# A new order for four engines between attention tile 4 and the first expert gathers

## The chip, the core and the metric

One Trainium2 chip, one of its cores. The core's engines are PE (TensorE, the matrix products), DVE (VectorE), ACT (ScalarE), POOL (GpSimd) and SP (SyncE, which only issues transfers here). Each runs its own list of instructions strictly in order, and semaphores tie the lists together. The metric is the device time of one execution in microseconds (us), as the median of several runs.

## The reference: cross-attention, then a mixture of experts

`x` is (2, 512, 128), 1024 tokens of 128 numbers; `ctx` is (2, 77, 128).

```
x = x + xattn(layernorm(x), ctx, W_q, W_kv, W_out, gamma, beta)     # 16 heads of 64
    xn  = layernorm(x) * gamma + beta
    q   = xn @ W_q / 8 ;  k, v = split(ctx @ W_kv)
    out = softmax(q k^T) v  per head, joined, @ W_out
x = x + ffn(layernorm(x), ...)                                      # 8 experts, top 2, d_ff 512
    probs = softmax(x @ Wg + bg);  the two largest per token, normalized to sum 1
    out   = sum over the two experts e of
            w_e * ((silu(x @ W1[e] + b1[e]) * (x @ W3[e] + b3[e])) @ W2[e] + b2[e])
```

All is float32. The kernel computes an expert only for the tokens that chose it.

## The kernel before

**Tiles.** The tokens form T = 8 tiles of 128, TB = 4 for each of the two batches. The weights are folded first: scores are `xn_tile @ g` (16 heads times 77 context rows, 1232 columns, 3 PSUM banks), and attention's output is `prob @ vo` with 1232 rows in CH = 10 chunks of 128.

**A tile of attention.** `score_mm(t)` (PE) writes the scores into banks 0 to 2 (even t) or 3 to 5 (odd t). DVE takes the negative maximum (L728) and subtracts (L733, semaphore `s_sub`), which frees the banks; ACT does the exponential (`exps`, L578); DVE sums and inverts (`sums`, L721, L724); POOL multiplies (L476, `s_norm`). PE transposes the ten chunks in groups of four, four and two (keys `("pT", t, i)`, L1246, `st_mm`); ACT copies each group into `probT[:, t % 2]` (L595, L598, `st_free`); PE multiplies the ten chunks with `vo` (L1261; float32 products show as two instructions each, 20 a tile) into a bank `y`. For tiles 0 to 4 ACT copies `y` out (L560) and POOL adds it to x (`add_x`, L468); for tiles 5 to 7 DVE adds it from PSUM (`add_direct`, L763) and takes the statistics at once.

**PSUM.** The list `stage` names everything that goes through banks 7 and 6 in turn: `pT` of a tile, then `y`. Tiles 5 and 6 have their `y` in banks 3 and 4 (`Y_OWN`). `open_stage` waits until ACT has emptied what was in a bank before.

**The router** works on three groups of tiles: 0 to 3, 4 to 5, 6 to 7. For group n:
- statistics of x2 (`ln_stats`, DVE), then `rstd_step(4 + n)` on POOL (an add, L456, and a power, L458);
- `tokens_x2T(n)` (PE, L1156) transposes x2, ACT copies (`empty_x2T`, L566), `logits(n)` (PE, L1165) multiplies with the centred router weights `wg_c`. The router's means and the expert biases are two small PE operations at the head of `tokens_x2T(0)`;
- on DVE `shifts(n)` (L770), `top_two(n)` (L778 to L793: logits, maxima, indices, masks, and `sel`);
- `count_ranks(n)` (PE, L1174 to L1181) counts, per expert, the tokens ahead of each one;
- on DVE `ranks(n)` (L801), `blocks_of(n)` (L811 to L815) and `one_hots(n)` (`perm`, L822).
- ACT writes the normalized tokens `xf` (`normed(n)`, L573), SP stores them to a DRAM scratch (L396).

After group 1, six of eight tiles are ranked. `full_blocks` and `first_tiles` (DVE, L836 to L855) find which tokens fill the first FULL = 5 expert tiles, whose 128 rows are complete whatever tiles 6 and 7 bring; `first_experts` (L861 to L864, `eid_1_ok`) finds their experts. `slot_rows` (PE, L1192) turns the hits into row numbers, DVE writes them to `idx` (L933, `idx_1_ok`). Then POOL gathers tokens by indirect DMA (`gather`, L501), and SP loads the weights of the first four expert tiles (L383) after `eid_1_ok`.

**Order.** It is written out by hand for each engine. PE before, for tiles 4 to 7: `pT(4)`, `tokens_x2T(0)`, products 4, `logits(0)`, `pT(5)`, products 5, `count_ranks(0)`, `pT(6)`, `tokens_x2T(1)`, `logits(1)`, products 6, `count_ranks(1)`, `pT(7)`, half of products 7, `slot_rows`, the other half, `tokens_x2T(2)`, `logits(2)`, `count_ranks(2)`, then the gathered transposes `expert_xT(0)` and `(1)` (L1203) and the first expert's products (`up(0)`, L1216). POOL: `add_x(4)`, the normalization of tile 7, `rstd_step(5)`, `rstd_step(6)`, gathers.

**Experts.** NT = 23 tiles of 128 gathered tokens; for each, two up-projections (L1216), silu on ACT (L647), a product on DVE (L956), the down-projection (L1227), bias (L965), a scatter (L510). At the end the rows come back in token order and are weighted (L997, L1000).

## Time and profile before

| What | Value |
|---|---|
| Median of 3 runs | 173.23 us (170.93 to 173.52) |
| Profiled execution, first to last instruction | 172.2 us |
| Profiled execution's own full time | not listed apart from the three runs |
| PE / PEld busy | 139.1 us (81%) / 129.1 us (75%) |
| DVE / ACT / POOL busy | 108.0 (63%) / 77.3 (45%) / 78.5 us (46%) |
| Chain that ended last | PE 59%, DMA 13%, DVE 12%, ACT 6% |

PE is the matrix engine's products, PEld its weight loads, which overlap the products. The chain that ended last is followed back from the last instruction, at each step to what released it. The page also divides the span into 40 slices of 4.3 us, with a digit for each engine's busy share in tenths and the granted TensorE clock in tenths of full speed. "L1216" is a line of the kernel.

### The profile page before, as it was taken

The numbers are of one execution on the slowest core, as the hardware profiler recorded it, in microseconds if no ns is written. First come the engines' busy times: TensorE is split into PE (matmuls) and PEld (weight loads), VectorE is DVE, ScalarE is ACT, GpSimd is POOL, SyncE is SP. The second block draws the span as 40 slices with busy tenths as digits, with TensorE's granted clock in tenths as the row PEclk, the third lists the DMA queues.
The fourth block names the chain that finished last, engine by engine and source line by source line (L and its number), as shares of the span: only waits on it lengthen the run. The fifth ranks groups of instructions, "written<-read, shape, count | busy, mean of one in ns | idle before, by whom it ended". The sixth has DMA issues, their size and how long they took to land.

```text
span 172.2 us, 3864 instructions
## 1 busy us (share of the span) xinstructions
PE 139.1 (81%) x1109; PEld 129.1 (75%) x1109; DVE 108.0 (63%) x354; ACT 77.3 (45%) x210; POOL 78.5 (46%) x98
## 2 busy tenths in 40 slices
PE   6499797999999979776149999999999999995000
PEld 6387685778999869665139989999999999994000
DVE  0685899988999963877843653535363545445074
ACT  3058467855745647450213543544545363535000
POOL 2650303944565680202740177777777763335000
PEclk9969999999999987998555999999999999999555
DMA  4999600030000000403990577787778686400453
GB/s 140 300 313 285 168 0 0 0 121 5 2 0 4 0 0 0 122 4 81 284 318 6 169 247 199 220 277 256 227 233 253 202 274 223 128 15 32 126 163 91
DMA packets 21629, 23.63 MB, mean 137 GB/s; under 512 B 2349, under 2 KB 14473, under 8 KB 21609
## 3 DMA queue, kind: packets, MB, share of 16 engines
q1 hardware_dynamic: 19300, 19.51, 37.8%
q0 software_dynamic: 1472, 3.02, 5.7%
q10 hardware_dynamic: 837, 0.87, 1.5%
q8 instruction: 9, 0.15, 0.4%
q14 instruction: 11, 0.09, 0.2%
HBM read 19.98 MB, written 3.41 MB: 136 GB/s over the span
## 4 chain that ended last, share of the span: by engine, by line
PE 59%; DMA 13%; DVE 12%; ACT 6%; issue 4%; POOL 2%; ACTq 1%; DVEq 0%; SPq 0%; POOLq 0%
PE psum L1216 22%; PE psum L1261 11%; PE psum L1227 10%; DMA early<-in_L_xattn_W_q_dram 5%; PE psum L1246 5%; DMA g_room<-xf_scratch,idx 5%; PE psum L1007 2%; PE psum L1009 2%; PE psum L1008 2%; DMA y_back<-y_scratch 2%; DVE prob L733 2%; DVE xn L1000 2%; DVE negmax L728 2%; PE psum L1203 2%; DVE x L997 1%
## 5 line engine op out<-in xcount | busy, mean ns | idle before, releaser
L956 DVE SCALAR_TENSOR_TENSOR probT<-psum,bias_col,prob 128x128 f32<-128x128 f32 x92 | 25.9, 344 | 35.5 <-ACT prob L647 30.6
L1216 PE MATMUL psum<-probT,w 128*128 128x128 f32 x368 | 47.4, 284 | 0.8 <-ACT probT L636 0.8
L1216 PEld LDWEIGHTS psum<-probT,w 128*128 128x128 f32 x368 | 45.3, 201 | 1.3 <-ACT probT L636 1.1
L647 ACT ACTIVATE prob<-psum,bias_col 128x128 f32<-128x128 f32 x92 | 26.3, 369 | 36.2 <-PE psum L1216 36.2
L501 POOL DMA_INDIRECT g_room<-xf_scratch,idx x23 | 22.4, 974 | 16.5 <-DVE idx L910 9.9
L476 POOL TENSOR_TENSOR prob<-prob,rowsum 128x1232 f32<-128x1232 f32 x8 | 18.0, 2249 | 15.3 <-DVE rowsum L724 15.3
L1227 PE MATMUL psum<-w,probT 128*128 x184 | 24.4, 276 | 0.0
L510 POOL DMA_INDIRECT y_scratch<-xnT,out_row x18 | 17.6, 978 | 14.5 <-DVE xnT L965 11.7
L1227 PEld LDWEIGHTS psum<-w,probT 128*128 128x128 f32 x184 | 22.3, 192 | 0.1
L1261 PE MATMUL psum<-vo,probT 128*128 128x128 f32 (+1 forms) x160 | 20.9, 288 | 0.0
L1261 PEld LDWEIGHTS psum<-vo,probT 128*128 128x128 f32 (+1 forms) x160 | 19.9, 204 | 0.3 <-ACT probT L595 0.3
L595 ACT ACTIVATE probT<-psum 128x512 f32<-128x512 f32 (+1 forms) x24 | 11.2, 490 | 13.0 <-PE psum L1246 12.9
L456 POOL TENSOR_SCALAR rstd<-mv 128x4 f32<-128x4 f32 (+1 forms) x7 | 1.8, 264 | 27.8 <-DVE mv L680 27.8
L1246 PE MATMUL psum<-ident,prob 128*128 128x128 f32 x80 | 12.6, 283 | 1.3 <-ACT probT L595 0.8
L728 DVE TENSOR_REDUCE negmax<-psum 128x16 f32<-128x1232 f32 x8 | 11.5, 1433 | 2.2 <-PE psum L1009 2.2
L733 DVE TENSOR_TENSOR prob<-psum,negmax 128x1232 f32<-128x1232 f32 x8 | 11.5, 1441 | 0.3
L721 DVE TENSOR_REDUCE rowsum<-prob 128x16 f32<-128x1232 f32 x8 | 11.3, 1418 | 0.2 <-ACT prob L578 0.2
L578 ACT ACTIVATE prob<-prob 128x1232 f32<-128x1232 f32 x8 | 9.8, 1226 | 2.9 <-DVE prob L733 2.9
L1246 PEld LDWEIGHTS psum<-ident,prob 128*128 128x128 f32 x80 | 8.6, 141 | 3.1 <-ACT probT L595 1.8
L1007 PE MATMUL psum<-g_room,xn_hi 128*128 128x512 f32 (+1 forms) x24 | 9.1, 379 | 1.3 <-issue 1.3
L1203 PE MATMUL psum<-ident,g_room 128*128 128x128 f32 x23 | 6.9, 298 | 3.2 <-DMA g_room<-xf_scratch,idx 3.1
L636 ACT ACTIVATE probT<-psum 128x128 f32<-128x128 f32 x23 | 6.7, 292 | 5.5 <-PE psum L1203 5.4
(162 smaller groups left out, 189.9 us busy)
## 6 DMA issues: line engine op xcount, KB each, us to landing
w<-in_L_ffn_W_dram SPq DMA_DIRECT2D x54, 256.0 KB, 4.8
early<-in_L_xattn_W_kv_dram SPq DMA_DIRECT2D x2, 512.0 KB, 7.6
y_back<-y_scratch SPq DMA_DIRECT2D x4, 256.0 KB, 3.7
early<-in_L_xattn_W_q_dram ACTq DMA_DIRECT2D x1, 512.0 KB, 9.1
early<-in_L_xattn_W_out_dram SPq DMA_DIRECT2D x1, 512.0 KB, 10.0
early<-in_L_ffn_b_dram SPq DMA_DIRECT2D x1, 512.0 KB, 3.8
xf_scratch<-xf SPq DMA_DIRECT2D x2, 256.0 KB, 2.6
xf_scratch<-xf SPq DMA_DIRECT2D x4, 128.0 KB, 3.5
```

Of the source, the lines that this page charges most:

```text
L476: pool.tensor_tensor(prob[:, t % NP_, :].rearrange("p (h m) -> p h m", h=H), prob[:, t % NP_, :].rearrange("p (h m) -> p h m", h=H), rowsu ...
L501: pool.indirect_dma_start(xg[:, j % GR, :], None, xf_dram[:, :], bass.IndirectOffsetOnAxis(ap=idx[:, j:j + 1], axis=0)).then_inc(xg_ok[j % ...
L510: pool.indirect_dma_start(y_dram[:, :], bass.IndirectOffsetOnAxis(ap=rows_of[:, j:j + 1], axis=0), y_sb[:, j % YR, :], None).then_inc(y_st ...
L647: act.activation(silu[:, j % 2, c, :], psum[:, 2 * (j % 2), c * P:(c + 1) * P], ACT.Silu, bias=bias_col[:, 0, bass.ds(expert, 1), c]).then ...
L728: dve.tensor_reduce(negmax[:, t, :], scores(t), AX.X, ALU.max, negate=True).then_inc(s_dve, 1)
L733: dve.tensor_tensor(heads(t), scores(t), negmax[:, t, :].rearrange("p (h o) -> p h o", o=1).broadcast_to([P, H, M]), ALU.add).then_inc(s_s ...
L956: dve.scalar_tensor_tensor(out=hT[:, j % 2, c, :], in0=psum[:, 2 * (j % 2) + 1, c * P:(c + 1) * P], scalar=bias_col[:, 1, bass.ds(expert[j ...
L1007: pe.matmul(dst, w_h, m_h, start=True, stop=False)
L1216: ins = pe.matmul(psum[:, 2 * (j % 2) + a, c * P:(c + 1) * P], w13[:, j % WR, a, c * P:(c + 1) * P], xt[:, j % XR, :], start=True, stop=True)
L1227: ins = pe.matmul(Y_AT[j % 2], hT[:, j % 2, c, :], w2[:, bass.ds(expert[j], 1), c, :].rearrange("p e d -> p (e d)"), start=(c == 0), stop= ...
L1246: ins = pe.transpose(bank[0:rows(c), k * P:(k + 1) * P], prob[:, t % NP_, c * P:c * P + rows(c)], ident[:, :])
L1261: ins = pe.matmul(bank[:, 0:P], probT[0:rows(c), t % 2, c, :], vo[0:rows(c), t // TB, c, :], start=(c == 0), stop=(c == CH - 1))
```

## The change

PE does the transposes of tiles 4 and 5 together, then x2's of group 0. For that the late transposes go to score banks that are free by then (`LATE`; `open_stage` waits for the last subtractions), and x2T of groups 0 and 1 to bank 3, of group 2 to bank 6. `router_means` comes before the transposes of tile 4. The products of tile 5 follow the router products of group 0 directly; count, x2T and router products of the next group are put between the transposes of tiles 6 and 7; `count_ranks(1)` stands in the middle of the products of tile 6; `slot_rows` comes after all products.

ACT copies tiles 4 and 5, then x2T of group 0, then y of tile 4. DVE writes the router weights and `shifts(0)` before the sums of tile 7, makes the masks and the ranked masks of a group in one operation each, splits the one-hots of group 0 in two halves around `top_two(1)`, and does `first_experts` right after `full_blocks`. POOL does `rstd_step(6)` after the second gather instead of before the first.

```diff
-        for t in range(T):
-            stage += [("pT", t, i) for i in range(len(pt_groups))]
-            if t not in Y_OWN:
-                stage += [("y", t)]
+        for t in [*range(TB), *range(TB, T, 2)]:
+            pair = [t] if t < TB else [t, t + 1]
+            stage += [("pT", k, i) for k in pair for i in range(len(pt_groups))]
+            stage += [("y", k) for k in pair if k not in Y_OWN]
...
         OWN = {("voT", 4): 3, ("voT", 5): 4}
+        LATE = {("pT", TB, 0): 7, ("pT", TB, 1): 6, ("pT", TB, 2): 2, ("pT", TB + 1, 0): 4, ("pT", TB + 1, 1): 5, ("pT", TB + 1, 2): 0,
+                ("y", TB): 7, ("pT", TB + 2, 0): 6, ("pT", TB + 2, 1): 2, ("pT", TB + 2, 2): 0,
+                ("pT", TB + 3, 0): 7, ("pT", TB + 3, 1): 6, ("pT", TB + 3, 2): 2, ("y", TB + 3): 0}
...
-            bank_of[key] = OWN[key] if key in OWN else rotation[0]
-            if key not in OWN:
+            bank_of[key] = OWN.get(key, LATE.get(key, rotation[0]))
+            if key not in OWN and key not in LATE:
...
-        XT_AT = [psum[:, 0, :], psum[:, 2, :], psum[:, 3, :]]
-        LG_AT = [psum[:, 1, 0:TB * E], psum[:, 2, 3 * P:3 * P + (FIRST - TB) * E], psum[:, 1, 2 * P:2 * P + (T - FIRST) * E]]
+        XT_AT = [psum[:, 3, :], psum[:, 3, :], psum[:, 6, :]]
+        LG_AT = [psum[:, 1, 0:TB * E], psum[:, 1, 2 * P:2 * P + (FIRST - TB) * E],
+                 psum[:, 1, 2 * P + (FIRST - TB) * E:2 * P + (T - TB) * E]]
...
-            for n in range(5, 4 + G):
+            for n in range(5, 4 + G - 1):
                 rstd_step(n)
...
             for j in range(AHEAD):
+                if j == 2:
+                    rstd_step(4 + G - 1)
                 gather(j)
...
-                if t + LAG_T < T:
-                    exps(t + LAG_T)
-                if t < T - 3:
-                    empty_stage(("y", t), y_out[:, t, :], stage_bank(("y", t))[:, 0:P])
-                if t == T - 4:
-                    empty_x2T(0)
-                elif t == T - 3:
-                    act.preload_act_table(ACT.Silu)
-                    normed(0)
-                elif t == T - 2:
-                    empty_x2T(1)
+
+            def empty_y(t):
+                empty_stage(("y", t), y_out[:, t, :], stage_bank(("y", t))[:, 0:P])
+
+            for t in range(TB):
+                empty_pT(t)
+                exps(t + LAG_T)
+                empty_y(t)
+            empty_pT(TB)
+            exps(TB + LAG_T)
+            empty_pT(TB + 1)
+            empty_x2T(0)
+            empty_y(TB)
+            act.preload_act_table(ACT.Silu)
+            normed(0)
+            empty_pT(TB + 2)
+            empty_x2T(1)
+            empty_pT(TB + 3)
             normed(1)
             empty_x2T(2)
             normed(2)
...
-            sums(T - 1)
-            dve.wait_ge(const_ok, 16)
-            dve.wait_ge(ld["router"], 32)
-            dve.wait_ge(mean_mm, 1)
-            dve.tensor_copy(bias_col[:, :, :, :].rearrange("p a e c -> p (a e c)"), BIAS_AT).then_inc(wg_ok, 1)
-            dve.tensor_tensor(wg_c[:, :], wg_sb[:, :], MEAN_AT, ALU.subtract).then_inc(wg_ok, 1)
...
-                for t in g:
-                    ins = dve.tensor_tensor(mask[:, t, :, :],
-                                            iota_e[:, :].rearrange("p (o e) -> p o e", o=1).broadcast_to([P, K, E]),
-                                            top_i[:, t, 0:K].rearrange("p (k o) -> p k o", o=1).broadcast_to([P, K, E]),
-                                            ALU.is_equal)
-                link(ins)
+                link(dve.tensor_tensor(mask[:, g.start:g.stop, :, :],
+                                       iota_e[:, :].rearrange("p (a o e) -> p a o e", a=1, o=1).broadcast_to([P, len(g), K, E]),
+                                       top_i[:, g.start:g.stop, 0:K].rearrange("p t (k o) -> p t k o", o=1).broadcast_to([P, len(g), K, E]),
+                                       ALU.is_equal))
...
-                for t in g:
-                    ins = dve.tensor_tensor(ranked[:, t, :, :], mask[:, t, :, :],
-                                            psum[:, RANK_BANK, t * E:(t + 1) * E].rearrange("p (o e) -> p o e", o=1)
-                                            .broadcast_to([P, K, E]), ALU.mult)
-                ins.then_inc(rk_read, 1)
+                dve.tensor_tensor(ranked[:, g.start:g.stop, :, :], mask[:, g.start:g.stop, :, :],
+                                  psum[:, RANK_BANK, g.start * E:g.stop * E].rearrange("p (t o e) -> p t o e", o=1, e=E)
+                                  .broadcast_to([P, len(g), K, E]), ALU.mult).then_inc(rk_read, 1)
...
-            def one_hots(n):
-
-                g = groups[n]
+            def one_hots(n, g=None):
+
+                last = g is None or g.stop == groups[n].stop
+                g = groups[n] if g is None else g
                 pairs = slice(g.start * K, g.stop * K)
-                dve.tensor_tensor(perm[:, pairs, :], iota_q[:, :].rearrange("p (o q) -> p o q", o=1).broadcast_to([P, len(g) * K, P]),
-                                  q_of[:, g.start:g.stop, :].rearrange("p t (k o) -> p (t k) o", o=1).broadcast_to([P, len(g) * K, P]),
-                                  ALU.is_equal).then_inc(perm_ok, 1)
+                ins = dve.tensor_tensor(perm[:, pairs, :], iota_q[:, :].rearrange("p (o q) -> p o q", o=1).broadcast_to([P, len(g) * K, P]),
+                                        q_of[:, g.start:g.stop, :].rearrange("p t (k o) -> p (t k) o", o=1).broadcast_to([P, len(g) * K, P]),
+                                        ALU.is_equal)
+                if last:
+                    ins.then_inc(perm_ok, 1)
...
+            dve.wait_ge(mean_mm, 1)
+            dve.tensor_copy(bias_col[:, :, :, :].rearrange("p a e c -> p (a e c)"), BIAS_AT).then_inc(wg_ok, 1)
+            dve.tensor_tensor(wg_c[:, :], wg_sb[:, :], MEAN_AT, ALU.subtract).then_inc(wg_ok, 1)
             shifts(0)
+            sums(T - 1)
+            dve.wait_ge(const_ok, 16)
+            dve.wait_ge(ld["router"], 32)
             top_two(0)
             late_stats(4)
             add_direct(5)
             ranks(0)
             blocks_of(0)
-            one_hots(0)
+            one_hots(0, range(0, TB // 2))
             shifts(1)
             top_two(1)
+            one_hots(0, range(TB // 2, TB))
             ranks(1)
             full_blocks()
+            first_experts()
             blocks_of(1)
             one_hots(1)
             first_tiles()
             add_direct(6)
-            first_experts()
             dve.wait_ge(idx_1_mm, 1)
             dve.tensor_scalar(idx[:, 0:FULL], FIRST_AT, row_base[:, 0:1], None, ALU.add).then_inc(idx_1_ok, 1)
             add_direct(7)
@@ -1090,11 +1104,13 @@
...
             def open_stage(key):
-                if before[key] and not (key in OWN and before[key][0] == "voT"):
+                if key in LATE and bank_of[key] < 6:
+
+                    pe.wait_ge(s_sub, T if bank_of[key] >= 3 else T - 1)
+                if key in OWN:
+                    pe.wait_ge(s_sub, 2)
+                elif before[key]:
                     pe.wait_ge(st_free, slot[before[key]] + 1)
-                elif key in OWN:
-
-                    pe.wait_ge(s_sub, 2 if key[0] == "voT" else T if OWN[key] >= 3 else T - 1)
                 return stage_bank(key)
...
+            def router_means():
+
+                pe.wait_ge(s_sub, T - 1)
+                pe.wait_ge(ld["router"], 32)
+                pe.wait_ge(const_ok, 16)
+                pe.matmul(MEAN_AT, mean_of[:, :], wg_sb[:, :], start=True, stop=True)
+                pe.wait_ge(ld["brows"], 32)
+                pe.transpose(BIAS_AT, bias_rows[:, :], ident[0:2 * BR, 0:2 * BR]).then_inc(mean_mm, 1)
+
             def tokens_x2T(n):
 
                 g = groups[n]
                 if n == 0:
                     pe.wait_ge(s_sub, T)
-                    pe.wait_ge(ld["router"], 32)
-                    pe.wait_ge(const_ok, 16)
-                    pe.matmul(MEAN_AT, mean_of[:, :], wg_sb[:, :], start=True, stop=True)
-                    pe.wait_ge(ld["brows"], 32)
-                    pe.transpose(BIAS_AT, bias_rows[:, :], ident[0:2 * BR, 0:2 * BR]).then_inc(mean_mm, 1)
+                elif n == 2:
+                    pe.wait_ge(st_free, slot[("pT", T - 1, 1)] + 1)
                 pe.wait_ge(x2_ok, g.stop)
-                if n == 2:
-                    pe.wait_ge(idx_1_ok, 1)
                 for k, t in enumerate(g):
                     ins = pe.transpose(XT_AT[n][:, k * P:(k + 1) * P], x2[:, t, :], ident[:, :])
...
                 pe.wait_ge(sel_ok, n + 1)
                 if n == 0:
+                    pe.wait_ge(st_free, slot[("pT", TB + 1, 1)] + 1)
...
-            pe.wait_ge(ld["router"], 32)
-            for t in range(T):
-                pe.wait_ge(s_norm, t + 1)
-                for i, g in enumerate(pt_groups):
+            def prob_T(t, i):
+
+                if i == 0:
+                    pe.wait_ge(s_norm, t + 1)
+                bank = open_stage(("pT", t, i))
+                for k, c in enumerate(pt_groups[i]):
+                    ins = pe.transpose(bank[0:rows(c), k * P:(k + 1) * P], prob[:, t % NP_, c * P:c * P + rows(c)], ident[:, :])
+                ins.then_inc(st_mm, 1)
+
+            def open_y(t):
+
+                if t == TB + 1:
+                    pe.wait_ge(xft_ok, 1)
+                elif t == TB + 2:
+                    pe.wait_ge(st_free, slot[("pT", TB + 1, 0)] + 1)
+                else:
+                    open_stage(("y", t))
+                return psum[:, Y_OWN[t], :] if t in Y_OWN else stage_bank(("y", t))
+
+            def attend(t, bank, chunks):
+
+                for c in chunks:
+                    if c % 4 == 0:
+                        pe.wait_ge(st_free, slot[("pT", t, c // 4)] + 1)
+                    ins = pe.matmul(bank[:, 0:P], probT[0:rows(c), t % 2, c, :], vo[0:rows(c), t // TB, c, :],
+                                    start=(c == 0), stop=(c == CH - 1))
+                if chunks.stop == CH:
+                    ins.then_inc(y_own if t in Y_OWN else st_mm, 1)
+
+            for t in range(TB):
+                for i in range(len(pt_groups)):
                     if i == len(pt_groups) - 1:
-                        if t + LEAD < T:
-                            score_mm(t + LEAD)
-                    bank = open_stage(("pT", t, i))
-                    for k, c in enumerate(g):
-                        ins = pe.transpose(bank[0:rows(c), k * P:(k + 1) * P], prob[:, t % NP_, c * P:c * P + rows(c)], ident[:, :])
-                    ins.then_inc(st_mm, 1)
-                if t == T - 4:
-                    tokens_x2T(0)
-                elif t == T - 2:
-                    tokens_x2T(1)
-                    logits(1)
-                bank = psum[:, Y_OWN[t], :] if t in Y_OWN else open_stage(("y", t))
+                        score_mm(t + LEAD)
+                    prob_T(t, i)
+                bank = open_y(t)
                 if t == 0:
                     pe.wait_ge(st_free, slot[("vo", len(vo_groups) - 1)] + 1)
-                for c in range(CH):
-                    if c % 4 == 0:
-                        pe.wait_ge(st_free, slot[("pT", t, c // 4)] + 1)
-                    if t == T - 1 and c == CH // 2:
-                        slot_rows(FIRST * K, hit_1, FIRST_AT, hit_1_ok, idx_1_mm)
-                    ins = pe.matmul(bank[:, 0:P], probT[0:rows(c), t % 2, c, :], vo[0:rows(c), t // TB, c, :],
-                                    start=(c == 0), stop=(c == CH - 1))
-                ins.then_inc(y_own if t in Y_OWN else st_mm, 1)
-                if t == T - 4:
-                    logits(0)
-                elif t == T - 3:
-                    count_ranks(0)
-                elif t == T - 2:
-                    count_ranks(1)
-
+                attend(t, bank, range(CH))
+            router_means()
+            for i in range(len(pt_groups)):
+                prob_T(TB, i)
+            for i in range(len(pt_groups)):
+                prob_T(TB + 1, i)
+            tokens_x2T(0)
+            attend(TB, open_y(TB), range(CH))
+            logits(0)
+            attend(TB + 1, open_y(TB + 1), range(CH))
+            for i in range(len(pt_groups)):
+                prob_T(TB + 2, i)
+            count_ranks(0)
+            tokens_x2T(1)
+            for i in range(len(pt_groups) - 1):
+                prob_T(TB + 3, i)
+            logits(1)
+            prob_T(TB + 3, len(pt_groups) - 1)
+            bank = open_y(TB + 2)
+            attend(TB + 2, bank, range(CH // 2))
+            count_ranks(1)
+            attend(TB + 2, bank, range(CH // 2, CH))
+            attend(TB + 3, open_y(TB + 3), range(CH))
+            slot_rows(FIRST * K, hit_1, FIRST_AT, hit_1_ok, idx_1_mm)
```

## Rows read from the trace of the kernel before

**Rows 1.** The chain of waits in order of time: start us, us, what.

```profile
50.91 1.02 PE psum L1246 x8
...
56.10 0.45 PE psum L1246 x4
...
58.57 2.25 PE psum L1261 x20
...
64.65 3.47 PE psum L1261 x20
...
75.79 0.69 DVE perm L822
...
81.09 0.71 POOL rstd L458
...
82.00 1.24 POOL g_room L501
...
83.55 4.33 DMA g_room<-xf_scratch,idx
...
89.23 3.77 PE psum L1216 x16
```

**Rows 2.** Stretches: busy us (and count) of PE, PEld, DVE, ACT, POOL; granted clock, DMA.

```profile
63.70:67.10 3.40, 3.15 (x16) 3.12 (x16) 1.81 (x18) 3.08 (x7) 0.35 (x1) 0.50 0.00 0
67.10:80.70 13.60, 10.70 (x102) 9.12 (x101) 10.21 (x52) 5.11 (x15) 0.95 (x2) 1.00 0.21 60
80.70:94.40 13.70, 7.36 (x34) 6.69 (x35) 7.64 (x40) 3.19 (x10) 6.01 (x7) 0.50 0.65 197
```

**Rows 3.** Timeline of PE: start us, us, line, operation [idle before <- releaser].

```profile
61.75 1.03 PE L1165 MATMUL psum<-wg_c,xfT 128*128 128x8 f32 x8 [0.95 <-ACT xfT L566]
...
68.21 1.07 PE L1246 MATMUL psum<-ident,prob 128*128 128x128 f32 x8
...
78.12 0.46 PE L1192 MATMUL psum<-hit,perm 128*128 128x5 f16 x12 [1.21 <-DVE hit L855]
```

**Rows 4.** Timeline of ACT around the evictions, exponential and normalizations.

```profile
56.57 1.40 ACT L595 ACTIVATE probT<-psum 128x512 f32<-128x512 f32 x3 [0.16 <-PE psum L1246]
...
58.03 1.23 ACT L578 ACTIVATE prob<-prob 128x1232 f32<-128x1232 f32 x1
...
61.02 0.59 ACT L566 ACTIVATE xfT<-psum 128x512 f32<-128x512 f32 x1
...
75.85 0.87 ACT L573 ACTIVATE xf<-x,shift,rstd 128x128 f32<-128x128 f32 x2
```

**Rows 5.** Timeline of POOL: the last tile's probability normalization.

```profile
61.80 2.25 POOL L476 TENSOR_TENSOR prob<-prob,rowsum 128x1232 f32<-128x1232 f32 x1
```

**Rows 6.** Timeline of DVE: the router steps.

```profile
65.03 0.19 DVE L793 TENSOR_TENSOR sel<-mask 128x32 f16<-128x32 f32 x1
...
68.15 0.29 DVE L763 TENSOR_TENSOR x<-x_sb,psum 128x128 f32<-128x128 f32 x1 [2.50 <-PE psum L1261]
...
71.32 0.15 DVE L770 SCALAR_TENSOR_TENSOR shift<-mv,rstd 128x2 f32<-128x2 f32 x1
...
73.89 0.25 DVE L801 TENSOR_TENSOR ranked<-mask,psum 128x16 f32<-128x16 f32 x2 [0.87 <-PE psum L1181]
...
78.72 0.15 DVE L861 TENSOR_TENSOR ended<-iota_j,bounds 1x40 f32<-1x40 f32 x1
...
79.21 0.20 DVE L933 TENSOR_SCALAR idx<-psum,row_base 128x5 uint32<-128x5 f32 x1
...
82.36 0.16 DVE L770 SCALAR_TENSOR_TENSOR shift<-mv,rstd 128x2 f32<-128x2 f32 x1
...
83.87 0.17 DVE L793 TENSOR_TENSOR sel<-mask 128x16 f16<-128x16 f32 x1
```

**Rows 7.** Timeline of SP's queue: the first four experts' weights.

```profile
80.25 5.56 SPq L383 DMA_DIRECT2D w<-in_L_ffn_W_dram  x8
```

**Rows 8.** Landing times of the 23 gathers (L501).

```profile
DMA to landing us min/median/max: 2.5/3.8/4.8
```

2 lines of the change are left out of this document (1 added, 1 removed).

## The prediction

> **What bounds the kernel now.** I read the page first: PE is the busiest engine, but its row of tenths falls to almost nothing shortly before the middle of the run, so there the bound is a chain. The chain of waits in order of time shows it. Up to 56.10 us it runs through PE, and from 89.23 us it is again PE, expert tile after expert tile [rows 1]. The change lies between. There the chain goes over PE (transposes, attention products, router products), then over DVE (ranks, one-hots, hits), once more over PE (the slot rows), then statistics, POOL's rstd, the first two gathers and their landing [rows 1]. Whatever makes the first expert product start earlier moves all that comes after, since one-hots of group 2, the other experts and the later gathers all hang on it. So the question is by how much 89.23 moves.
>
> Three things in that stretch cost time. First, at 61.75 PE had waited 0.95 us for ACT's copy of x2T, and then the granted clock fell to 0.50 from 63.70 to 67.10 [rows 2, 3]. The 20 attention products of tile 5 took 3.47 us there against 2.25 us for tile 4 [rows 1]. Second, PE waited 1.21 us for the hits before the slot rows at 78.12 [rows 3]. Third, the row numbers of the first gathers were written by 79.41 (79.21 + 0.20) [rows 6], but the first gather began at 82.00, because POOL's queue holds the rstd step of group 2 ahead of it, which ended at 81.80 [rows 1]. That is 2.59 us during which the gathers had all they needed from DVE.
>
> **The change, from 56.10 us on.** One full-clock transpose is 0.128 us (8 in 1.02) [rows 1]; ten make 1.28.
>
> *PE to the end of tile 5.* Router means and bias transpose now go first; nothing gives their time alone here, I bound it between 0 and three transposes, 0.38, and take 0.3. Two tiles of transposes 2.56 and four transposes of x2 0.51 bring PE to 59.5; the products of tile 4 (2.25) to 61.75. They need probT of tile 4. ACT needs 1.46 us per tile (56.57 to 58.03) and starts when the first group lands at 56.9, so it is done at 58.4: hidden. ACT goes on with the exponential of tile 7 (1.23), tile 5's copies (1.46) and x2T (0.59) [rows 4], ending at 61.7. So the router products of group 0 start at 61.8, where they started before at 61.75, but PE no longer waits for them: there is a gap of under 0.1 us instead of 0.95. They take 1.03 [rows 3]. Tile 5 follows at once, 62.8 to 65.1 at full clock; before it ended at 68.1 (64.65 + 3.47) [rows 1]. Of these 3.0 us, 1.2 are the clock, the rest is the transposes and their wait taken out from between.
>
> *Router group 0.* sel of group 0 was written at 65.22 before [rows 6]. It keeps its place, since y(4) and the sums of tile 7 fit into DVE's wait for the router products; four mask operations in one save at least 0 and at most 0.4, I take 0.2. Add and statistics of tile 5 cost about 0.8 (an estimate from the add of 0.29 [rows 6] and as much again for statistics and aggregation) and end at 66.3. PE does the transposes of tile 6 (1.28) and the count of group 0 by 66.6. DVE's later ranks, block arithmetic and the first half of the one-hots follow. Before, 3.17 us passed from the add's start (68.15) to the shift of group 1 (71.32), with a one-hot of 1.22 [rows 6]; half a one-hot is 0.69, the size of the four-pair one in rows 1. So the shift comes 2.6 after the add's new start of 65.5, plus about 0.4 for the count, at 68.5: 2.8 earlier. POOL meanwhile normalizes tile 7 only after add_x(4), so from 62.5 instead of 61.80, 2.25 long [rows 5]; at 64.8 it is done, and PE asks for it at 66.9. Here 2 us of cover are left.
>
> *Group 1.* PE has its x2 transposes at 66.9, two thirds of tile 7's transposes by 67.9, its router products by 68.5, so DVE does not wait. From shift to sel a two-tile group takes 1.7 us (82.36 to 84.04) [rows 6]: 70.1, then the second half of the one-hots, 0.69: 70.8. PE runs the first half of tile 6's products and the count by 70.3. So DVE starts the ranks of group 1 at 70.8, not 73.89 [rows 6]: 3.1 earlier. The experts' step, 0.57 (78.72 to 79.29) [rows 6], now comes ahead of the hits, and the merged rank operation gives back 0 to 0.1. PE has only 3.4 us of products left (one and a half tiles) against DVE's 4.8, so it waits longer for the hits than before, about 1.9 us instead of 1.21; that wait costs nothing by itself, since DVE is the path. The hits are ready at 75.5 instead of 78.07. Slot rows 0.46 [rows 3] run beside add_direct(6), then idx is written by 76.5: 2.9 earlier than 79.41.
>
> *POOL and the gathers.* With rstd behind two gathers, the first can start 0.2 to 0.3 us after idx, at 76.7 (before: 82.00), 5.3 earlier. It also needs the stores of groups 0 and 1. Group 1's normalization started at 75.85 before [rows 4]; it follows the shift (2.8 earlier) and tile 7's copies, so about 69.2 to 70.1, and POOL has six microseconds over. The price: rstd(2) is queued behind two issues of 1.55 us (82.00 to 83.55) [rows 1] and ends about 1.05 later, at 80.9; at least its pow of 0.71 [rows 1] and the add before it. DVE then takes 1.7 to sel at 82.4, and PE's count of group 2 stands ahead of the first gathered transpose. That transpose could have started at 81.2 and waits until 82.6. With the copy of ACT between, the second starts at 83.4, not at its landing (78.25 + 4.33 = 82.6 [rows 1]). Before, the first product began 1.35 us after that landing (89.23 against 87.88); so it begins at 84.7, bounds 83.9 (nothing lost to the count) and 85.4. DVE's other tiles end near 87.0 and are needed only after the first expert's products, 3.77 long [rows 1], at 88.5: cover of 1.5 us.
>
> **Sum.** 89.23 - 84.7 = 4.5, and from the pieces: 2.9 (idx) + 2.4 (the wait for rstd) - 0.8 (the new queue behind it). The rest of the run is the same work in the same order. The profiled execution has a span of 172.2 us, so 167.7; its own full time is not listed, the span stands 1.0 below the median of 173.23, and I take the difference from the median: **168.7 us**, 2.6% less. A measurement of this kernel tells about 2% from no change, here 3.5 us.
>
> **Clock, weighed.** From 68.11 to 71.44 PE did transposes, four small router products and counts, no attention products, and the granted clock stayed at 1.00 through that stretch [rows 2, 3]. So transposes seem to hold the clock, and the change's 24 in a row are harmless.
> By the Trainium skill (TensorE: Matmul & The Clock Gate, PE-mode transpose) transposes do not count as activity for the clock gate; by that rule the packed transposes would drop the clock for tiles 4 and 5, and the trace speaks against it.
>
> **Rivals.**
> (a) The clock falls for one tile anyway. For it: the router products still stand between tiles 4 and 5, where it fell last time. Against: PE's gap there is gone. Price 3.47 - 2.25 = 1.2: 169.9. Chance 15%.
> (b) The long run of transposes lets it fall for tiles 4 and 5, each 1.2: 171.1. Chance 6%. This is the place of the rule above.
> (c) The first gathers land late. eid is now ready some four microseconds ahead of idx, so the weights of four experts (5.56 us of issues from 80.25 [rows 7]) are in full flow when the gathers start. For: the first landings took 4.33, the worst of 23 took 4.8 [rows 8]. Against: before, the weights ran beside the same gathers. Up to 4.8 is hidden by the wait for sel; at 6 it would cost 1.2: 169.9. Chance 9%.
> (d) The packed order doesn't come about: PE or ACT stops on a freed bank or a copy, tile 5 and group 0 stay where they were, and only POOL's new order is left, 2.4 - 0.8: 171.6. Against: the last subtraction from score banks 3 to 5 ends before PE asks for them. Chance 7%.
> (e) Slower. POOL's queue now puts rstd(2), thus sel, the count and both gathered transposes, behind gather 0. From gather 0's start to the first expert product it was 7.23 (82.00 to 89.23), and becomes 8.0. If group 1's stores came so late that gather 0 started after 81.2, the run would be slower than before. The place is SP's store behind ACT's normalization; if that stayed at 75.85 plus 0.87 and took 6 us to issue and land, gather 0 would start at 82.7 and the run be 174.7. Nothing in the rows keeps it there. Chance 3%.
>
> **Numbers.** Forecast as summed: 60%, own range 167.5 to 169.7 from the bounds of the first product (0.8 earlier, 0.7 later) and some tenths of scatter. Range for 8 in 10: 166.9 to 170.9; it takes in (a), (c), and most of (b)'s lower side, leaving (d), (e) and the tails. Faster by over 2% means under 169.77: nearly all of the forecast and a little under half of (a) and (c): 0.68. Slower by over 2% (above 176.7): 0.02. The rest 0.30.
>
> **What would show it.** In the changed kernel's profile: 24 probability and x2 transposes in a row and a gap under 0.2 us before the group 0 router products; tile 5's products in about 2.3 us at clock 1.00; DVE's ranks of group 1 near 70.8; PE waiting near 1.9 us for the hits; the first gather within 0.3 us of idx, near 76.7; POOL's rstd of two tiles after the second gather; the first gathered transpose waiting on the count, not on its DMA; the first expert product near 84.7. A clock of 0.50 in tiles 4 to 7, a gather landing after 6 us, or a wait of PE on ACT's copies would make it wrong.

## The result, and the profile after

The changed kernel takes **167.44 us** in the median of 4 runs (166.45 to 168.23), the kernel before 172.69 us in the runs beside it (170.93 to 173.52). The ratio is **0.971**, 95% interval 0.9658 to 0.9762: 2.9% faster, 5.0 us by the ratio (the two medians lie 5.25 apart). Forecast were 168.7 us, a range of 166.9 to 170.9, and 68% for faster by over 2%. The profiled execution has a span of 166.2 us within a time of 168.23 us.

The stretches of the changed kernel; columns as in [rows 2]:

```profile
56.00:62.40 6.40, 6.33 (x57) 6.08 (x55) 4.84 (x12) 5.56 (x13) 4.62 (x6) 1.00 0.00 0
62.40:64.80 2.40, 2.40 (x23) 2.40 (x23) 2.05 (x19) 2.23 (x5) 2.02 (x1) 1.00 0.00 0
64.80:75.50 10.70, 8.43 (x91) 7.92 (x89) 9.50 (x48) 3.89 (x11) 0.95 (x2) 1.00 0.41 124
76.00:86.00 10.00, 5.05 (x25) 4.27 (x24) 6.39 (x34) 2.47 (x8) 5.85 (x7) 0.50 0.61 209
...
94.50:96.10 1.60, 0.32 (x4) 0.13 (x3) 1.12 (x4) 0.69 (x3) 1.29 (x2) 1.00 0.82 314
```

The granted clock stays at 1.00 from 56 to 75.5 us. In [rows 2] it was 0.50 from 63.70 to 67.10. Between 56 and 96 us it falls only once, at 76.0, among PE's waits between the hits and the first expert product, and it is back at 86.2.

PE in the changed kernel: start us, us, line, operation, and in brackets the idle time before it with what ended it.

```profile
56.29 2.40 PE L1264 MATMUL psum<-ident,prob 128*128 128x128 f32 x20
58.53 0.60 PE L1176 MATMUL psum<-ident,x 128*128 128x128 f32 x4
...
61.43 1.03 PE L1185 MATMUL psum<-wg_c,xfT 128*128 128x8 f32 x8
62.32 2.48 PE L1282 MATMUL psum<-vo,probT 128*128 128x128 f32 x20
...
67.78 1.28 PE L1282 MATMUL psum<-vo,probT 128*128 128x128 f32 x10
69.49 0.19 PE L1200 MATMUL psum<-sel,ones 128*128 128x40 f16 x1 [0.42 <-DVE sel L799]
...
69.60 3.59 PE L1282 MATMUL psum<-vo,probT 128*128 128x128 f32 x30
74.59 0.46 PE L1213 MATMUL psum<-hit,perm 128*128 128x5 f16 x12 [1.40 <-DVE hit L862]
...
81.13 0.45 PE L1224 MATMUL psum<-ident,g_room 128*128 128x128 f32 x1
82.04 0.45 PE L1224 MATMUL psum<-ident,g_room 128*128 128x128 f32 x1 [0.46 <-DMA g_room<-xf_scratch,idx]
83.15 3.47 PE L1237 MATMUL psum<-probT,w 128*128 128x128 f32 x16 [0.66 <-ACT probT L650]
...
96.09 0.33 PE L1224 MATMUL psum<-ident,g_room 128*128 128x128 f32 x1 [1.28 <-DVE probT L970]
```

The last row names DVE as what ended the wait. But this transpose takes a gathered tile, the sixth, and the weight load that belongs to it shows the gather (PEld):

```profile
96.09 0.14 PEld L1224 LDWEIGHTS psum<-ident,g_room 128*128 128x128 f32 x1 [1.47 <-DMA g_room<-xf_scratch,idx]
```

Twenty transposes of the probabilities and four of x2 stand in a row, the router products start at 61.43 with no gap worth naming (it was 0.95 [rows 3]), and tile 5's products are done at 64.80, against 68.11 [rows 1]. The slot rows start at 74.59 (78.12 in [rows 3]) after 1.40 us of waiting, and the first expert product at 83.15 (89.23 in [rows 1]).

DVE (its answer to [rows 6]) and POOL:

```profile
64.63 0.19 DVE L799 TENSOR_TENSOR sel<-mask 128x32 f16<-128x32 f32 x1
...
67.28 0.69 DVE L827 TENSOR_TENSOR perm<-iota_q,q_of 128x512 f16<-128x512 f16 x1
67.89 0.15 DVE L778 SCALAR_TENSOR_TENSOR shift<-mv,rstd 128x2 f32<-128x2 f32 x1
...
69.95 0.18 DVE L806 TENSOR_TENSOR ranked<-mask,psum 128x32 f32<-128x32 f32 x1
...
70.95 0.19 DVE L868 TENSOR_TENSOR ended<-iota_j,bounds 1x40 f32<-1x40 f32 x1
...
74.32 0.22 DVE L862 TENSOR_TENSOR hit<-hit,val 128x60 f16<-128x60 f16 x1
...
75.20 0.19 DVE L947 TENSOR_SCALAR idx<-psum,row_base 128x5 uint32<-128x5 f32 x1
...
79.38 0.16 DVE L778 SCALAR_TENSOR_TENSOR shift<-mv,rstd 128x2 f32<-128x2 f32 x1 [1.49 <-POOL rstd L462]
...
80.77 0.17 DVE L799 TENSOR_TENSOR sel<-mask 128x16 f16<-128x16 f32 x1
```

```profile
62.17 2.25 POOL L480 TENSOR_TENSOR prob<-prob,rowsum 128x1232 f32<-128x1232 f32 x1
...
75.69 1.24 POOL L505 DMA_INDIRECT g_room<-xf_scratch,idx  x1 [8.62 <-DVE idx L947]
77.23 0.95 POOL L505 DMA_INDIRECT g_room<-xf_scratch,idx  x1 [0.30 <-issue]
78.21 0.26 POOL L460 TENSOR_SCALAR rstd<-mv 128x2 f32<-128x2 f32 x1
78.55 0.73 POOL L462 TENSOR_TENSOR rstd<-rstd,neg_half 128x2 f32<-128x2 f32 x1
...
91.86 0.95 POOL L505 DMA_INDIRECT g_room<-xf_scratch,idx  x1 [8.78 <-DVE idx L917]
```

idx is written 0.3 us before gather 0 starts, where it had waited 2.6 us for rstd. The rstd step stands behind gather 1 and ends at 79.28.

**One measure for all traces.** Tile 3's products end at another moment in each execution (between 54.3 and 57.1 us in the 14 profiled ones), since the part before scatters. So the table counts from that end, S: the start of L1261's or L1282's last group before 57 us, plus its duration, less 0.14 us by which a product outlasts the next one's start. Each kernel's trace gives slot rows, gather 0 (G) and the first expert product (U):

| Kernel | S to slot rows | slot rows to G | G to U | U to end | S to end | ratio to before (95%) |
|---|---|---|---|---|---|---|
| before | 22.2 | 3.9 | 7.2 | 83.0 | 116.2 | 1 |
| changed | 18.7 | 1.1 | 7.5 | 83.1 | 110.3 | 0.971 (0.966 to 0.976) |
| changed, again (e9) | 18.7 | 1.1 | 7.4 | 82.8 | 110.1 | 0.971 (0.965 to 0.977) |
| e1 rstd alone | 21.0 | 2.9 | 7.9 | 83.5 | 115.3 | 0.989 (0.983 to 0.995) |
| e4 gap filled | 21.0 | 3.9 | 7.0 | 82.9 | 114.8 | 0.998 (0.994 to 1.002) |
| e2 rstd first | 18.7 | 2.9 | 7.0 | 82.9 | 111.5 | 0.974 (0.967 to 0.980) |
| e3 gap put back | 19.6 | 1.1 | 7.6 | 82.8 | 111.1 | 0.974 (0.969 to 0.979) |
| e5 experts late | 18.2 | 1.6 | 7.6 | 82.7 | 110.1 | 0.976 (0.970 to 0.982) |
| e10 unmerged | 19.0 | 1.1 | 7.5 | 82.4 | 110.0 | 0.973 (0.967 to 0.978) |
| e11 unsplit | 19.1 | 1.1 | 7.5 | 82.3 | 109.9 | 0.973 (0.968 to 0.979) |
| e6 other rows early | 18.7 | 1.1 | 7.6 | 81.5 | 108.9 | 0.966 (0.960 to 0.972) |
| e12, the same again | 18.7 | 1.1 | 7.6 | 82.2 | 109.5 | 0.962 (0.957 to 0.967) |
| e7 one gather | 18.7 | 1.1 | 6.3 | 83.8 | 109.9 | 0.979 (0.972 to 0.985) |
| e8 both | 18.7 | 1.1 | 6.5 | 82.3 | 108.6 | 0.966 (0.960 to 0.972) |

The first column is to be noticed: where the order on DVE and PE and the clock are the same, it agrees to 0.05 us from execution to execution. A whole run scatters by 1 to 2 us; this stretch does not. Every column but the ratio is read from one execution.

### The profile page after: what moved, and what is told of

It is laid out like the page before. It is cut to its first block, busy times and chain, and to the rows that moved or that the text cites. A ratio compares the mean times of both kernels' runs of the same rounds, so it can differ in the third digit from the quotient of the medians.

```text
span 166.2 us, 3861 instructions
## 1 busy us (share of the span) xinstructions
PE 135.3 (81%) x1109; PEld 127.1 (76%) x1109; DVE 107.1 (64%) x345; ACT 76.6 (46%) x210; POOL 78.9 (47%) x98
## 4 chain that ended last, share of the span: by engine, by line
PE 63%; DVE 13%; DMA 10%; ACT 6%; issue 3%; POOL 1%; SPq 1%; ACTq 0%; POOLq 0%; DVEq 0%
PE psum L1237 25%; PE psum L1248 11%; PE psum L1282 8%; PE psum L1264 5%; DMA early<-in_L_xattn_W_kv_dram 4%; DMA g_room<-xf_scratch,idx 3%; PE psum L1021 2%; PE psum L1023 2%; PE psum L1089 2%; PE psum L1022 2%; DMA y_back<-y_scratch 2%; PE psum L1224 2%; DVE prob L747 2%; DVE xn L1014 2%; DVE negmax L742 2%
## 5 line engine op out<-in xcount | busy, mean ns | idle before, releaser
L1237 PE MATMUL psum<-probT,w 128*128 128x128 f32 x368 | 46.5, 281 | 0.7 <-ACT probT L650 0.7
L1237 PEld LDWEIGHTS psum<-probT,w 128*128 128x128 f32 x368 | 44.4, 197 | 1.3 <-ACT probT L650 0.9
L1248 PEld LDWEIGHTS psum<-w,probT 128*128 128x128 f32 x184 | 22.3, 192 | 0.1
L1282 PE MATMUL psum<-vo,probT 128*128 128x128 f32 (+1 forms) x160 | 19.3, 276 | 0.0
L1282 PEld LDWEIGHTS psum<-vo,probT 128*128 128x128 f32 (+1 forms) x160 | 18.5, 192 | 0.0
L1264 PE MATMUL psum<-ident,prob 128*128 128x128 f32 x80 | 11.3, 276 | 0.4 <-ACT vo L601 0.4
L1021 PE MATMUL psum<-g_room,xn_hi 128*128 128x512 f32 (+1 forms) x24 | 9.1, 379 | 1.3 <-issue 1.3
L1023 PE MATMUL psum<-g_room,xn_hi 128*128 128x512 f32 (+1 forms) x24 | 8.5, 355 | 0.0
L1022 PE MATMUL psum<-g_room,xn_lo 128*128 128x512 f32 (+1 forms) x24 | 8.5, 355 | 0.0
```

What stands on the lines that cost most here:

```text
L1021: pe.matmul(dst, w_h, m_h, start=True, stop=False)
L1237: ins = pe.matmul(psum[:, 2 * (j % 2) + a, c * P:(c + 1) * P], w13[:, j % WR, a, c * P:(c + 1) * P], xt[:, j % XR, :], start=True, stop=True)
L1248: ins = pe.matmul(Y_AT[j % 2], hT[:, j % 2, c, :], w2[:, bass.ds(expert[j], 1), c, :].rearrange("p e d -> p (e d)"), start=(c == 0), stop= ...
L1264: ins = pe.transpose(bank[0:rows(c), k * P:(k + 1) * P], prob[:, t % NP_, c * P:c * P + rows(c)], ident[:, :])
L1282: ins = pe.matmul(bank[:, 0:P], probT[0:rows(c), t % 2, c, :], vo[0:rows(c), t // TB, c, :], start=(c == 0), stop=(c == CH - 1))
```

## The experiments

The experiments came in three groups of four, e1 to e4, e5 to e8 and e9 to e12. Each group ran beside its own runs of the kernel before, and each ratio is to those.

**e1, rstd alone.** The kernel before with POOL's order changed:

```diff
-            for n in range(5, 4 + G):
+            for n in range(5, 4 + G - 1):
                 rstd_step(n)
...
             for j in range(AHEAD):
+                if j == 2:
+                    rstd_step(4 + G - 1)
                 gather(j)
```

> The kernel before, with POOL's rstd of group 2 moved behind the second gather and nothing else. My theory (the gathers waited for rstd, and the new queue behind them gives part of it back): gather 0 starts 0.3 us after idx, near 79.7 instead of 82.0, and the first expert product 7.5 us later (as in the changed kernel, 75.69 to 83.15), near 87.2 instead of 89.2: about 2.0 us faster, ratio 0.988. Rival: the landing of the second gather decides, and with the weights of the first experts issued only then it lands more than 5 us after its issue; then 1.0 us or less is gained, ratio 0.994 or above.

Measured: 170.77 us, ratio 0.989. Its profile does not show the 2 us: from S to the first product it took 31.7 us, and 31.9 in e4, which has POOL's old order and the same clock up to there. The chain of waits of e1 tells why (start us, us, what):

```profile
74.16 0.77 ACT xf L575 x2
...
74.95 0.36 SPq L396
...
75.35 2.98 DMA xf_scratch<-xf
...
79.21 1.24 POOL g_room L501
...
82.08 0.73 POOL rstd L458
...
84.65 0.20 PE psum L1181
...
84.92 0.33 PE psum L1205
...
85.69 0.46 PE psum L1205
...
87.06 3.12 PE psum L1218 x13
```

Gather 0 did not wait for idx (written by 77.61) but for the landing of group 1's stores at 78.33: ACT normalized at 74.16, SP issued at 74.95, and the transfer took 2.98 us. From there sel, the count and the copies set the first product. The second gather's landing, the rival, is not on the chain. So in the old order this edit by itself is held by the stores. In this execution PE also waited 0.81 us before the sixth gathered transpose, and from S to the end it is not shorter than e4 (115.3 against 114.8). Where the time of the median (2.1 us below that of before) comes from is open; the kernel's own six executions reach from 170.1 to 172.4, and the profiled one is of the slow end (172.3).

**e2, rstd first again.** The changed kernel with the two places of e1 turned back:

```diff
-            for n in range(5, 4 + G - 1):
+            for n in range(5, 4 + G):
...
-                if j == 2:
-                    rstd_step(4 + G - 1)
```

> The changed kernel with POOL's rstd of group 2 back ahead of the gathers. My theory: gather 0 waits for rstd and starts near 77.5 instead of 75.7, and the first expert product comes 7.2 us later, near 84.7 instead of 83.15: 1.6 us slower than the changed kernel, some 169.0 us, ratio to before 0.979. Rival: the gathers are bound by the weights' transfers, which end at the same time either way; then the first product moves by under 0.7 us and the ratio stays near 0.973. The rest of the gain against before (2.1%) is then what the new order of PE, ACT and DVE is worth.

Measured: 168.62 us, ratio 0.974. In the trace gather 0 starts 2.9 us after the slot rows instead of 1.1 and the product follows 7.0 later instead of 7.5: 1.3 us, between the 1.6 expected and the rival's 0.7, nearer to mine. The times show 0.4 us (0.9735 against 0.971), and their interval takes in both theories. Note that 2.9 is 1.0 less than before: with all of tile 7's products ahead of the slot rows, add_direct(7) follows idx at once, and so does rstd.

**e3, the gap put back.**

```diff
-            empty_x2T(0)
-            empty_y(TB)
+            empty_y(TB)
+            empty_x2T(0)
```

> The changed kernel with one exchange on ACT: y of tile 4 is copied out before x2T of group 0. PE then waits about 1.0 us for that copy ahead of the router products of group 0, as it did in the kernel before (0.95 us). If that gap made the granted clock fall to 0.50 for the products of tile 5, they take 3.5 us again and idx comes 2.2 us later: about 169.6 us, ratio 0.983. If the gap alone doesn't do it, the clock stays at 1.00, tile 5 takes 2.3 us, and the cost is 1.0 us: 168.4, ratio 0.976.

Measured: 168.13 us, ratio 0.974. PE waited exactly the 0.95 us of [rows 3], and the clock did not fall:

```profile
60.74 1.03 PE L1185 MATMUL psum<-wg_c,xfT 128*128 128x8 f32 x8 [0.95 <-ACT xfT L572]
61.62 2.48 PE L1282 MATMUL psum<-vo,probT 128*128 128x128 f32 x20
...
73.90 0.46 PE L1213 MATMUL psum<-hit,perm 128*128 128x5 f16 x12 [1.40 <-DVE hit L862]
```

Tile 5 took 2.48 us, the slot rows came 0.88 later. In this execution the gap did not bring the clock down; it cost its own length.

**e4, the gap filled in the kernel before.**

```diff
                 if t == T - 4:
+                    for _ in range(8):
+                        pe.transpose(psum[:, RANK_BANK, 3 * P:4 * P], ident[:, :], ident[:, :])
                     logits(0)
```

> The kernel before, with eight transposes of the identity into a free part of bank 5 while PE waits for the copy of x2T of group 0 (gap of 0.95 us filled; their results are overwritten). If the gap made the clock fall, and transposes hold it, tile 5's products take 2.3 us at clock 1.00 instead of 3.5, and the run is 1.2 us faster: ratio 0.993. If transposes don't hold the clock, it falls as before and nothing changes: ratio 1.000.

Measured: 172.31 us, ratio 0.998, no change. In its profile tile 5 took 2.40 us at full clock. That proves nothing, for in e1, with the gap not filled and the old order of PE, it did so too:

```profile
61.12 1.03 PE L1167 MATMUL psum<-wg_c,xfT 128*128 128x8 f32 x8 [0.95 <-ACT xfT L568]
...
63.60 2.40 PE L1263 MATMUL psum<-vo,probT 128*128 128x128 f32 x20
...
76.32 0.46 PE L1194 MATMUL psum<-hit,perm 128*128 128x5 f16 x12 [1.21 <-DVE hit L857]
```

So the low clock in tile 5 in [rows 1] and [rows 2] belongs to that execution, at least in part. Of three traces of the old order of PE one has it (in one of the other two the gap is filled), of eleven of the new order none. That is too few to say whether the new order takes the fall away or chance did. In the trace that has it the slot rows come 22.2 us after S, in the two others 21.0: there the fall cost 1.2 us. What it is worth in the median is not shown. Of the fourteen runs of before that the comparison with e1 to e4 uses, the seven with a mean clock of 0.915 or less have a median of 173.2 us, the seven above it 172.1. But the mean clock of a whole run does not tell of tile 5: it is 0.903 in the profile of before, which has the fall, and 0.904 in that of e5, which has none there but a low stretch from 12.0 to 18.9 us.

**e5, first_experts late again.** 

```diff
             full_blocks()
-            first_experts()
...
             add_direct(6)
+            first_experts()
             dve.wait_ge(idx_1_mm, 1)
```

> The changed kernel with first_experts back behind add_direct(6), so that hits, idx and the first gather come up to 0.57 us earlier and the first four experts' weights are asked for about 4 us later. My theory (the landing of the second gather, 4.69 us from its issue, is what the first expert product waits for, and the weights' transfers lie beside it either way): gather 0 near 75.2, the first product some 0.3 to 0.6 us earlier than 83.15, ratio 0.969. Rival: with the weights issued late, the first product waits for them or the gathers land later among them: the first product 1 us or more later, ratio 0.977 or above; then the early first_experts is part of the gain.

Measured: 167.91 us, ratio 0.976. Hits 0.5 earlier, as expected; but standing between add_direct(6) and idx the three operations cost the same again, and gather 0 comes 19.8 us after S in both. My expectation of an earlier gather was wrong by its own edit. What it does show: the weights' first issue moved from 16.6 us after S to 20.3 (72.52 and 77.42 in the two traces), and the first product hardly moved (27.4 us after S against 27.3). The early expert numbers are worth nothing here that the trace shows. The times do not settle it: 0.976 lies nearer to the rival's 0.977 than to the 0.969 expected, and the interval (0.970 to 0.982) takes in both 0.971 and a loss of over 1 us.

**e10, masks unmerged, and e11, one-hots whole and the count behind tile 6.** e10 puts the loops over tiles back:

```diff
-                link(dve.tensor_tensor(mask[:, g.start:g.stop, :, :],
+                for t in g:
+                    ins = dve.tensor_tensor(mask[:, t, :, :],
...
-                dve.tensor_tensor(ranked[:, g.start:g.stop, :, :], mask[:, g.start:g.stop, :, :],
+                for t in g:
+                    ins = dve.tensor_tensor(ranked[:, t, :, :], mask[:, t, :, :],
```

e11:

```diff
-            one_hots(0, range(0, TB // 2))
+            one_hots(0)
...
-            one_hots(0, range(TB // 2, TB))
...
-            attend(TB + 2, bank, range(CH // 2))
-            count_ranks(1)
-            attend(TB + 2, bank, range(CH // 2, CH))
+            attend(TB + 2, bank, range(CH))
+            count_ranks(1)
```

> The changed kernel with the masks and ranked masks in one operation per tile again. By the rows, a group of four cost 0.43 and 0.38 instead of 0.23 and 0.22, one of two 0.26 and 0.25 instead of 0.19 and 0.18. Theory: only group 1's sel and its ranks lie on the chain to the hits, so the slot rows come 0.1 to 0.4 us later, and group 2's sel 0.1 later: 0.2 to 0.5 us in all, ratio 0.972 to 0.974. Rival: each instruction costs more than its row on a busy DVE; slot rows over 0.6 us later.

> The changed kernel with group 0's one-hots in one operation ahead of top_two(1), and the count of group 1 after all of tile 6's products instead of amid them. Theory: DVE is the path either way, one-hots of 1.22 us stand ahead of sel and none behind it, so the ranks of group 1 start only 0.3 to 0.4 us later and so do the slot rows: ratio 0.973. The other 2.3 us by which the slot rows came earlier are then the products of tile 5 and the router products that no longer stand behind transposes. Rival: the mid-tile count is what brought group 1 forward; slot rows 1 us or more later, ratio 0.977.

Measured: slot rows 0.33 later in e10 and 0.36 in e11, as both theories had it; ratios 0.973 and 0.973. From S to the end neither is slower than the changed kernel (110.0 and 109.9), since U to end is 0.7 shorter in both: PE waited 0.39 and 0.26 us for the sixth gather there, and 1.28 in the changed kernel's profile. How long that gather takes to land differs between executions: 3.2 us from its issue in e11 (91.72), some 4.2 in the changed kernel's profile. With e3's 0.88 less the 0.5 of first_experts (e5), 0.33 + 0.36 + 0.88 - 0.5 = 1.1 of the 2.3 us by which the slot rows come earlier at the same clock (21.0 to 18.7), if the four add. The other 1.2 should be the transposes of tile 5 and their waits, which no longer stand between its router products and its attention products, and those of tile 6; that part follows by subtraction and was not undone by itself.

**e9, the changed kernel again**, beside e10 to e12.

> The changed kernel once more, on the chip and beside the same runs of before as the next three. If the clock's fall in tile 5's products is not a matter of this kernel's gap but of the execution, it can show here too; by all traces so far of this order (four with no gap, one with a gap of 0.95 us) it does not: tile 5 in 2.3 to 2.5 us. Ratio 0.971; slot rows 18.3 us and first expert product 26.9 us after the first transpose of tile 4.

Measured: 167.09 us, ratio 0.971 again; 18.7 and 27.2 us after S; tile 5 in 2.48 us. PE did not wait for the sixth gather by more than 0.3 us in this execution.

**e6 and e12, the other rows early.** The sixth gather waits for the second table of row numbers (`idx` of the other tiles, L917). In the changed kernel it starts at 91.86, and PE waits 1.28 us before 96.09 (stretch 94.5 to 96.1: PE busy 0.32 of 1.60). The edit:

```diff
+            one_hots(2)
             for j in range(NT + 1):
                 if j < NT:
                     gated(j)
-                if j == 0:
-                    one_hots(2)
-                if j >= 1 and j != 1:
+                if j >= 1:
                     bias_down(j - 1)
                 if j == 0:
+                    other_rows()
                     other_experts()
-                elif j == 1:
-                    other_rows()
-                    bias_down(0)
...
-                if j == 1:
+                if j == 0:
                     slot_rows(T * K, tile_hit, OTHER_AT, hit_ok, idx_mm)
```

> The changed kernel; one-hots of group 2, the slot rows of the other tiles and their idx come right after the first expert's products instead of after the second's. In the changed kernel PE waited 1.28 us for the sixth gather (95.0 to 96.1), which started only at 91.86. My theory: that wait ate what the earlier return of the clock gave; here the sixth gather starts near 88.3 and PE no longer waits: 1.0 to 1.3 us faster than the changed kernel, ratio 0.965. Rival: the wait is set by the transfers (weights and gathers together), not by idx, and the time does not move: 0.971.

> The version with the other rows right after the first expert's products, beside the changed kernel in the same call. If its gain of 1.4 us in the traces (first transpose of tile 4 to the end: 108.5 against 109.9) is real in the times too, its ratio is 0.007 to 0.009 below that of the changed kernel; if the first comparison was chance, the two agree within 0.003.

Measured: 166.82 us (0.966), then 165.88 us (0.962). Beside the second stands e9, the changed kernel, with 167.09 us (0.971); the first has only its runs of before beside it. POOL in e6, the sixth gather:

```profile
89.62 0.95 POOL L505 DMA_INDIRECT g_room<-xf_scratch,idx  x1 [5.64 <-DVE idx L917]
```

It starts 5.5 us after the first product instead of 8.7, and PE runs on without a wait: U to end is 81.5 and 82.2 against 83.1 and 82.8. In e12 the first two experts' products ran 5.7 us at half clock, and from S to the end it is still shorter than both traces of the changed kernel (109.5 against 110.3 and 110.1). Both ratios came as expected, 0.965 and 0.007 to 0.009 below the changed kernel; the intervals of e12 and e9 overlap (0.957 to 0.967, 0.965 to 0.977), so the gain of 1.2 us is likely and not certain. The wait of 1.28 us itself is one execution's: the trace of e9 has almost none, so what e6 and e12 take away is in part a chance of waiting, with a sixth gather that has 3 us more to land. It is not all: e9 and e12 both have no such wait and a clock that came back equally late (5.5 and 5.7 us after the first product), and e12 is 0.6 us shorter from there to the end. Where that part comes from is open.

**e7, one gather, and e8, both.** PE starts the first expert's products after one gathered transpose; e8 adds e6.

```diff
-            count_ranks(2)
...
             expert_xT(0)
-            expert_xT(1)
+            count_ranks(2)
...
                     up(j)
+                if j == 0:
+                    expert_xT(1)
...
# ACT
             expert_xT(0)
-            expert_xT(1)
...
                 gate_silu(j)
+                if j == 0:
+                    expert_xT(1)
```

> The changed kernel; PE starts the first expert's products after the first gathered transpose alone (count of group 2 behind it), and the second gathered transpose comes after them. The first gather landed before 81.1 where the second landed at 81.92. My theory: the first product starts 1.0 to 1.6 us earlier, near 81.8; of it at most half is seen at the end, since the sixth gather's idx decides later (its chain moves with the first product, but the clock may come back later): ratio 0.966 to 0.970. Rival: the first weights or the copy behind ACT's normalizations decide, and nothing is gained: 0.971.

> The two edits together: other rows right after the first expert's products, and the first product after one gathered transpose. If both theories hold they add: 1.5 to 2.5 us faster than the changed kernel, ratio 0.957 to 0.963. If only the early other rows matter: 0.965. If neither: 0.971.

Measured: 168.77 us (0.979, interval 0.972 to 0.985) and 166.52 us (0.966). The first product did come 1.15 us earlier in e7 (6.3 after G, not 7.5), and all of it was given back behind it: U to end grew by 0.75 to 1.0. PE in e7:

```profile
79.70 0.45 PE L1225 MATMUL psum<-ident,g_room 128*128 128x128 f32 x1 [3.00 <-DMA g_room<-xf_scratch,idx]
...
81.00 3.75 PE L1238 MATMUL psum<-probT,w 128*128 128x128 f32 x16 [0.73 <-ACT probT L650]
84.55 0.42 PE L1225 MATMUL psum<-ident,g_room 128*128 128x128 f32 x1
85.43 0.35 PE L1225 MATMUL psum<-ident,g_room 128*128 128x128 f32 x1 [0.46 <-ACT probT L650]
86.21 2.02 PE L1238 MATMUL psum<-probT,w 128*128 128x128 f32 x16 [0.44 <-ACT probT L650]
```

Two transposes with ACT's copies between them now stand in the middle of dense work, with 0.46 and 0.44 us of waits. In the trace of e7 gain and loss cancel; that its median lies 1.3 us above the changed kernel's the trace does not show, for the profiled execution is the fastest of its runs (166.81). An earlier start of the experts is no gain while their second link is late. e8 does not beat e6 and e12: 0.966, 0.966 and 0.962.

## Why the prediction was right

**PE up to tile 5** was right in mechanism and nearly in size: router products at 61.43 (61.8), tile 5 done at 64.80 (65.1). Ten transposes in a long row take 1.17 us (20 in 2.33), not 1.28, and the router's two small operations 0.32 (0.3). DVE did not wait where I said it would not; sel of group 0 by 64.82 (65.0).

**Clock.** The step that credited 1.2 us of clock to the change by closing the gap is not borne out. e1 and e3 have the gap and full clock, in one trace each. The forecast sum was made against one execution that had the low stretch; at equal clock the first product is 4.6 us earlier after S (31.9 in e4, 27.3 after), and 6.0 against the profile shown. Without its 1.2 us for the clock the forecast sum is 3.3 us, where 4.6 were measured at equal clock: that the sum of 4.5 came out so near is luck, of a credit that was not earned and of an idx counted short by nearly as much (below).
With twenty-four transposes in a row, four of them of x2, the granted clock stayed at 1.00, and so it did with those of tiles 6 and 7 and the router products between them. Rival (b) did not come, nor (a) in any of eleven traces.
By the Trainium skill (TensorE: Matmul & The Clock Gate, PE-mode transpose) a transpose does not count as busy time for the clock gate in the way a product does. The traces here disagree for float32 transposes and a row of this length, 2.8 us: the clock is at 1.00 behind it in all eleven. No run has a longer row.

**Router group 1.** The ranks began at 69.95 (70.8), the hits were ready at 74.54 (75.5). The times add up: tile 5's add began 0.3 us before its forecast (65.16, 65.5), from there to the shift of group 1 it took 2.7 us instead of 3.0 (DVE waited 0.21 us for the count, not 0.4), from the shift to the ranks 2.1 instead of 2.3, to the hits 4.6 instead of 4.7, and idx was written by 75.39 (76.5). So idx came 4.0 us earlier than in the profile of before, not 2.9; at equal clock, against e1 (22.3 us after S, and 19.5 in the changed kernel), it came 2.8 us earlier, where the forecast without its clock term says 1.7. This term was off by 1.1 us. Mask merges and the split have the small prices I gave them (0.33 and 0.36 in the runs). PE waited 1.40 us for the hits (1.9).

**POOL.** Gather 0 began 0.30 us after idx, at 75.69 (76.7), and group 1's stores were long in. The price of the new queue was mis-sized: 0.8 forecast, 0.2 to 0.5 measured, for G to the first product grew from 7.23 to 7.46 only (7.0 in e2 and e4). The error is in POOL's issues. I took 1.55 us for each of two, so that rstd would end 4.2 us after G; but the second took 0.98 us to where rstd began (77.23 to 78.21), and rstd ended 3.6 us after G. From there it went nearly as forecast: count done at 81.1, the first gathered transpose behind it. The second then had two things to wait for that ended together: the second gather landed at 81.92, 4.69 us from its issue at 77.23, and ACT's copy of the first transpose ended at 81.90, so the trace does not show that the landing cost anything. The chain at this place, and that copy:

```profile
75.69 1.24 POOL g_room L505
...
77.23 4.69 DMA g_room<-xf_scratch,idx
...
82.04 0.46 PE psum L1224
...
82.53 0.29 ACT probT L650
...
83.15 3.47 PE psum L1237 x16
```

```profile
81.62 0.28 ACT L650 ACTIVATE probT<-psum 128x128 f32<-128x128 f32 x1 [1.16 <-PE psum L1224]
```

What I gave to POOL's order alone (1.6) is 1.3 in e2, in the new order. In the old order, e1, it is held by the stores: the place of rival (e), which cost 1.3 us there (gather 0 at 79.21, where idx alone allowed 77.9) and did not turn the sign. The changed kernel escapes it because the stores of group 1 also moved: normalized from 68.31.

**The rest as before** was right in number (83.05 after the first product, 82.97 before) only by a balance. The prediction had nothing of the clock or of waits there. The clock returned 3.1 us after the first product instead of 5.2 (94.42 and 89.23 in the profile of before), and the sixth gather took the gain back with 1.28 us of waiting. In e9 the clock came back late (half speed until 87.2, 5.5 us after the first product), there was hardly a wait, and the sum was nearly the same (82.8): two things of one size, of which each execution of the changed kernel showed one.

**The total.** At equal clock the first product comes 4.6 us earlier: 2.8 (idx) + 2.3 (the wait for rstd) - 0.5 (the new queue). Undone one by one, POOL's order (e2), the gap (e3), the masks (e10) and the split with the count (e11) move it by 1.3, 1.0, 0.3 and 0.4 us, 3.1 of the 4.6 if they add; the other 1.5 rest on subtraction. Against the profile with the low clock it is 6.0. The measured 5.0 lies between, and how it divides is open, since nothing shows how many runs of before had the fall. (c) and (d) did not come: the first two gathers took 4.45 and 4.69 us beside the weights, under the 4.8 that (c) called hidden (5.05 for the second in e3, with 7.6 us from G to the first product), and no bank or copy stopped PE in the stretch of attention.
